# One unread product of 512 columns in front of the score products of every second step of the second attention

## The reference, cut to what matters

```python
x = x + _L0_xattn_ref(_layernorm(x), ctx_1024, ctx_1024, ...)   # first attention
x = x + _L0_ffn_ref(_layernorm(x), ...)                         # 8 experts, two per token
x = x + _L1_xattn_ref(_layernorm(x), ctx_1024, ctx_1024, ...)   # second attention: the change is here
x = x + _L1_ffn_ref(_layernorm(x), ...)                         # 8 experts, one per token

def _L1_xattn_ref(q, k, v, Wq, bq, Wk, bk, Wv, bv, Wo, bo):     # 4 x 512 x 256, 16 heads of 16
    qw = split_heads(q @ Wq + bq)
    kw = split_heads(k @ Wk + bk)
    vw = split_heads(v @ Wv + bv)
    scores = jnp.einsum('bhqd,bhkd->bhqk', qw, kw) * inv_sqrt_d
    weights = jax.nn.softmax(scores, axis=-1)
    ctx = jnp.einsum('bhqk,bhkd->bhqd', weights, vw)
    return ctx.transpose(0, 2, 1, 3).reshape(B, S, D_MODEL) @ Wo + bo
```

## Time and profile before

| what | value |
|---|---|
| median of 3 runs | 1158.53 us (1160.39, 1146.82, 1158.53) |
| the profiled execution | 1146.98 us |
| its span, first to last instruction | 1145.2 us |
| granted clock of TensorE, mean over the span | 0.919 |
| PE busy in the span | 975.3 us (85%) |
| DVE busy | 742.6 us (65%) |
| ACT busy | 478.4 us (42%) |
| second attention, first to last score product | 713.3 to about 998 us |

### The profile page before, as it was taken

The page is one execution under the profiler, slowest core; times in us unless marked ns, Lnnn a source line. Parts: engine busy times, 40 slices in busy tenths (PEclk is TensorE's granted clock), DMA queues, the critical chain, the costliest instruction groups (busy, mean ns, idle before and its releaser), DMA issues.

```text
span 1145.2 us, 20649 instructions
## 1 busy us (share of the span) xinstructions
PE 975.3 (85%) x6905; PEld 588.1 (51%) x6905; DVE 742.6 (65%) x1952; ACT 478.4 (42%) x1055; POOL 283.5 (25%) x248
## 2 busy tenths in 40 slices
PE   6878789878898799999998876888989897877993
PEld 3555455646465388878885432333333332335662
DVE  3474677684978766666663467687677856446665
ACT  3443725442343334433442310446665666532331
POOL 0334434523320233444321111100010011112551
PEclk8999989997998899999999997779998998887997
DMA  9442020003435311111114486323073014061225
GB/s 290 148 129 95 16 72 4 19 1 92 130 110 166 128 65 51 48 53 49 52 40 147 122 148 122 74 39 75 2 120 65 3 57 128 20 201 34 79 76 175
DMA packets 69506, 98.64 MB, mean 86 GB/s; under 512 B 6528, under 2 KB 56960, under 8 KB 66976
## 3 DMA queue, kind: packets, MB, share of 16 engines
q1 hardware_dynamic: 59808, 62.18, 19.0%
q0 software_dynamic: 9600, 35.14, 12.0%
HBM read 70.10 MB, written 27.13 MB: 85 GB/s over the span
## 4 chain that ended last, share of the span: by engine, by line
PE 49%; DVE 27%; DMA 10%; ACT 6%; issue 4%; POOL 2%; SPq 1%; DVEq 0%; POOLq 0%; ACTq 0%
PE pb L993 11%; PE pb L1010 7%; DVE MX L1932 5%; PE pb L1098 4%; PE pb L1011 3%; DMA QS<-qd 3%; PE pb L1122 3%; PE pb L758 2%; PE pb L1076 2%; PE pb L827 2%; PE pb L781 2%; PE pb L837 2%; DMA xr<-rows,gi 2%; DVE TQ L1541 1%; PE pb L1153 1%
## 5 line engine op out<-in xcount | busy, mean ns | idle before, releaser
L1355 ACT ACTIVATE m<-pb,b1m 128x128 f32<-128x128 f32 x404 | 115.1, 368 | 172.2 <-PE pb L993 172.1
L1932 DVE TENSOR_REDUCE MX<-pb 128x1 f32<-128x512 f32 x256 | 158.6, 684 | 43.7 <-PE pb L1076 43.3
L1412 ACT ACTIVATE EX<-pb 128x512 f32<-128x512 f32 x256 | 136.9, 598 | 115.4 <-PE pb L1122 114.5
L993 PE MATMUL pb<-xt,w1h 128*128 128x128 f16 x1616 | 157.6, 221 | 3.9 <-issue 2.7
L1010 PE MATMUL pb<-w,mh 128*128 x404 | 149.5, 380 | 5.4 <-DVE ml L1843 4.9
L752 PE MATMUL pb<-identh 128*128 128x512 f16 x558 | 136.6, 401 | 15.5 <-DVE UZ L1577 8.8
L993 PEld LDWEIGHTS pb<-xt,w1h 128*128 x1616 | 120.3, 98 | 42.5 <-issue 6.1
L993 PE MATMUL pb<-xt,w1l 128*128 128x128 f16 x808 | 112.8, 221 | 0.0
L1011 PE MATMUL pb<-w,ml 128*128 x404 | 110.2, 273 | 0.0
L2144 POOL DMA_INDIRECT outs<-ob,di x62 | 61.4, 990 | 174.3 <-DVE ob L1858 174.3
L752 PEld LDWEIGHTS pb<-identh 128*128 128x128 f16 x558 | 55.4, 102 | 87.4 <-issue 18.9
(11 more groups left out here) (319 smaller groups left out, 1598.0 us busy)
## 6 DMA issues: line engine op xcount, KB each, us to landing
SR<-in_w1m SPq DMA_DIRECT2D x20, 512.0 KB, 4.3
SR<-in_w2m SPq DMA_DIRECT2D x14, 512.0 KB, 4.8
GB<-outs SPq DMA_DIRECT2D x12, 512.0 KB, 6.9
KS<-kd SPq DMA_DIRECT2D x48, 128.0 KB, 5.6
QS<-qd POOLq DMA_DIRECT2D x24, 256.0 KB, 10.1
SRW<-in_w2m SPq DMA_DIRECT2D x10, 512.0 KB, 5.3
kd<-KHL POOLq DMA_DIRECT2D x8, 512.0 KB, 6.6
vd<-VAB POOLq DMA_DIRECT2D x4, 1024.0 KB, 4.4
```

The lines of the kernel that those rows point to most:

```text
L993: ins = pe.matmul(k.ap[:, h4 * TOK:(h4 + 1) * TOK], wt[:, bass.ds(regs[j], 128)], M.xt[j % 2][:, xc, :], start=i == 0, stop=i == 5)
L1355: ins = act.activation(M.m32[x % 2][:, h4, :], k.ap[:, h4 * TOK:(h4 + 1) * TOK], M.func, bias=M.b1[:, bass.ds(reg + 4 * g + h4, 1)], scale ...
L1412: act.activation(EX[m % len(EX)][:, i, :], k.ap, ACT.Exp, scale=0.25).then_inc(k.out, 1)
L1932: v.tensor_reduce(mx[:, t, 2 * s + j:2 * s + j + 1], k.ap, AX.X, ALU.max).then_inc(k.out, 1)
```

## The change: what it does

In front of the score products of every second step (n = 0, 2, ... 30) one unread product is issued, in all four batches: 64 products more on TensorE, nothing on any other engine. The product waits for the same S2 bank as the score product behind it.

```diff
@@ -1116,6 +1116,8 @@
                     if n == 0:
                         fill(S2, (14, 0, 0, 0)[b])
                     w.wait_ge(sem(f"d_qm{b % 2}{g // 2}"), 32 * (b // 2 + 1))
+                    if n % 2 == 0:
+                        fill(S2, 1)
                     for j in range(2):
                         k = S2.take()
                         w.wait_ge(*k.before)
```

## The result

The changed kernel takes 1160.55 us (median of 13 runs, 1159.74 to 1166.53). The kernel before, run beside it, takes 1149.58 (13 runs, 1135.84 to 1160.39). The ratio is 1.0153, with a 95% interval of 1.0128 to 1.0179: slower by 1.5%, and inside 2%. The three runs that the prediction had to go by stood at 1158.53, 9 us above the median of the thirteen.

What follows compares the result with a forecast made beforehand. TensorE bounds the second attention, VectorE close behind. Of 24.9 us price, 12.5 us hidden leaves about 12.5; less 8 us of clock, +4.5: 1151.5 or 1163.0 by base, middle taken as 1157 us, range 1142 to 1173.

Steps and rivals of the forecast that it cites:

- The sum itself: Whole change: 12.5 us paid on the path minus 8 us of clock returned, +4.5 us; main forecast's chance 0.42.
- The price of a product: Second attention on TensorE: 0.45 us at 26 places between two pairs, 0.27 us at 38 behind a full product.
- Cutting two pairs apart: At the 26 places between score pairs: parting the pairs costs 0.19 us, 0.41 to 0.50 us with the product itself.
- The 0.1 us for a change: On TensorE, each change between a full product and a pair was said to cost 0.1 us extra.
- the eight places that the forecast had at the lower clock: Eight of the 64 places, in stretches at the lower clock, cost double: 2.9 us more, 24.9 us in all.
- What is hidden: TensorE's idle time in the second attention hides 12.5 us of the added products, leaving about 12.5 us paid.
- 3 us for the waits for ScalarE's exponentials: Taken off 15.5 us that could be hidden, since exponentials start later too; such waits total 6.4 us over the stage.
- The clock: Added products keep or restore TensorE's upper clock in the second attention: 8 us won, half of 16.2 us.
- The rival 'the clock is not moved': Products cost their price and the clock's falls stay: +12.5 us, middle 1165 us, chance 0.25.
- The rival that saves the clock: Most of five clock falls in the second attention go away: -6.8 us, middle 1146 us, chance 0.22.
- the slower stretch with L1153: Batch 1 stretch without idle time, L1153 between pairs: should be longer by 0.3 to 0.5 us for each product.
- the 15 named: Prediction counts as wrong if the second attention's length, 285 us, moves by more than 15 us either way.

## Why the prediction was wrong

**The number.** The forecast was within 2% with 0.90 and a time of 1157 in 1142 to 1173; 1160.55 lies there. But 1157 is below the 1158.53 known then, so it was a forecast of a small gain, and the kernel is slower by 11 us, clear of the noise. The sum itself had the sign right, +4.5 us (the terms give 4.4). It was put between two bases, the profiled execution and the median of three runs, and that let the base decide the sign. The base was off as well: three runs of a kernel whose single runs differ by 25 us gave 1158.5 where thirteen gave 1149.6. The middle of the two bases, 1152.8, was 3 us too high and the sum nearly 7 too low; that these offset each other in part, and 1157 came within 4 us, is luck.

**The price of a product,** 0.45 and 0.27 us, measured 0.52 and 0.32. The range of the second was missed by a hundredth, that of the first by two. Cutting two pairs apart was priced from two lone pairs, and what the pair behind the added product costs extra was left out: at this clock 25.7 us instead of 22.0. The 0.1 us for a change, read from L1153, doesn't stand: its four products take the same 1.06 us to an `av` (the two lines below, of the kernel before) as to a pair, and the 0.86 us that they were set against is no row of L1153. Two corrections belong to the 25.7 us: 0.8 us less for the eight places behind L758 and L942, and about 2.2 us more for the eight places that the forecast had at the lower clock (it put 2.9). That makes about 27.1 us to set against its 24.9. The 131 ns of the Trainium skill (page "TensorE: Matmul & The Clock Gate", section "Back-to-back issue gap") are not seen in the timelines: a second product at a place takes 0.22 us, a single one behind `av` 0.32.

```profile
804.63 1.13 PE L1153 MATMUL pb<-Wqkv,XTR 128*128 128x256 f32 x4
805.69 1.07 PE L1098 MATMUL pb<-EX,VA 128*32 128x512 f32 x8
```

**What is hidden,** 12.5 us. In measured terms 27.1 - 16.5 = 10.6 us. The total is 2 us short, but here the mechanism failed. By batches the smaller of idle time and price had given 6.4 us in the first, 5.8 in the middle two and 3.3 in the last; measured on the same footing are about 5.9, 2.0 and 3.2. The middle batches' idle time was taken as cover and hid little. Of the idle time I had deducted 3 us for the waits for ScalarE's exponentials, which makes up for most of this in the total, and that was luck: one of these waits hid a product whole (793.54 above). The wait for VectorE's last maxima ahead of their transpose I had counted as cover; it depends on TensorE's own products and moved along whole, 4.6 us in both traces. An idle stretch hides added work only if what ends it does not follow from the work behind the addition. This is read from the two traces and agrees with what the middle batches pay, 10.9 us; no run took that wait away.

**The clock,** 8 us: 19 us less at the lower level, worth 0.28 us each, 5.3 us. The mechanism was right, as far as means can tell; in the stage of the traces it is 0.87 to 0.91, as the forecast had it. Its worth was taken as 0.30 per us (16.2 of 54.1), which the runs confirm; how much comes back was taken too large, and it doesn't come back in proportion: parts of the products gave +24, -8, -5, +2 and 0.

**The sum in measured terms:** 27.1 - 10.6 - 5.3 = 11.2 us, against 24.9 - 12.5 - 8 = 4.4. Of the 6.8 between them 2.2 are the price, 1.9 the idle time that hides nothing and 2.7 the clock. All three erred to the same side, and none stands out, as each is known to 1 or 2 us only. The rival 'the clock is not moved' had the size nearly right, +12.5, for another reason, since the clock did move. The rival that saves the clock named a real effect, which shows most in the first batch (0.95 with products at every step). Of what should show it, the slower stretch with L1153 came as told (0.52 against 0.3 to 0.5), the stage moved by 12.6, under the 15 named. PE's busy time rose by about 13 us in the stage, as it was to do if the clock is not moved, while the clock rose to 0.91. VectorE's maxima have 36.7% of the chain of waits in the first batch, and had 35.4%.

## What to carry to other kernels

A product that nobody reads can pay only where it keeps the clock up and another engine is late: here it came out even in the first batch and lost in the middle two. Count as cover only idle time whose end does not depend on the work that the addition delays. If products are added for the clock, look at where they stand: the first one at a place cost the most here, since it parts pairs of products that run close together, and a second one beside it cost next to nothing net. And measure a kernel that swings between clock levels with a dozen runs and fit time against clock before believing a difference of 1%.

## What was new about the hardware

Between pairs of products in the two halves of the rows, the next pair starts 0.34 us later; with a full product between, the two steps are 0.43 and 0.32, and the pair behind takes 0.44 to what follows instead of 0.33. The lower clock can last long in full work: 58 and 68 us in one piece, with PE busy 84 of 89 and 87 of 91 us in that batch, in the two kernels where the four products behind full ones were missing from that batch or, like all the others, had a quarter of their columns. The changed kernel's runs lie within 7 us of each other (13 runs), those of the kernel before within 25: more products made the time steadier as well as longer. And two single executions, of two different kernels, ran at a mean clock of 0.64 and 0.55, some 230 and 420 us longer than their neighbours; nothing here says why.
